# Two weighted sums of a graph network on one core: two stages with a barrier between them, against one stage with one list of tile pieces

## The reference

```python
h = (feat - mean) * rsqrt(var + EPS) * gamma + beta
feat_in, feat_out = h @ W_in + b_in, h @ W_out + b_out
a_in  = segment_sum(feat_in[src] * iw[:, None], dst, num_segments=N)
a_out = segment_sum(feat_out[dst] * ow[:, None], src, num_segments=N)
a = concatenate((a_in, a_out), axis=1)
xi, hh = a @ W_x2i + b_x2i, h @ W_h2h      # then gates: sigmoid, tanh, and the new h
```

## Time and profile before

| what | value |
|---|---|
| time, median of 3 runs | 4573.53 us (4573.35 to 4581.63) |
| the profiled execution, its own time | 4598.33 us |
| its span in the trace | 4596.4 us |
| TensorE busy | 3570.8 us, 78% of the span |
| VectorE / ScalarE / GpSimd busy | 58% / 37% / 23% |
| first sum (`gin`), matmuls | 265.3 us busy, 3674.53 us to 3939.8 us |
| second sum (`gou`), matmuls | 264.6 us busy, 3947.39 us to 4212.0 us |

### The profile page before, as it was taken

One profiled execution on the slowest core, in us unless ns is written; L12 is line 12 of the kernel. 1 busy time (PEld: TensorE's weight loads), 2 busy tenths in 40 slices (PEclk: granted clock), 3 DMA queues, 4 the chain that ended last, 5 costly groups with the idle time before them and its releaser, 6 DMA issues. The chain is left out here.

```text
span 4596.4 us, 88449 instructions
## 1 busy us (share of the span) xinstructions
PE 3570.8 (78%) x19416; PEld 2680.7 (58%) x19417; DVE 2671.9 (58%) x9145; ACT 1684.3 (37%) x5377; POOL 1077.8 (23%) x828
## 2 busy tenths in 40 slices
PE   5555548888777776999994433688999699998978
PEld 4333337776777775888883222677887344444444
DVE  7999989999887772101227888777765300000523
ACT  1555542333334441000008886777775100000110
POOL 1888888888882000000000000000000000000000
PEclk9999999999988888999995555899999899999989
DMA  3444434566667664444437654544331153542064
GB/s 104 111 111 114 111 76 126 148 187 203 193 192 246 237 242 123 134 136 127 134 98 208 188 178 130 160 126 129 112 100 61 59 210 114 179 149 66 1 256 138
DMA packets 435572, 656.94 MB, mean 143 GB/s; under 512 B 97532, under 2 KB 291767, under 8 KB 435362
## 3 DMA queue, kind: packets, MB, share of 16 engines
q1 hardware_dynamic: 354306, 526.63, 37.0%
q10 hardware_dynamic: 53040, 121.95, 7.3%
q0 software_dynamic: 28144, 7.36, 2.5%
HBM read 438.84 MB, written 216.02 MB: 142 GB/s over the span
## 5 line engine op out<-in xcount | busy, mean ns | idle before, releaser
L989 POOL DMA_INDIRECT slots<-all_B,put_index x800 | 1054.4, 1318 | 342.8 <-issue 240.4
L1724 POOL DMA_DIRECT2D out_dram<-all_B x7 | 8.6, 1224 | 2170.4 <-DVE all_B L1708 2170.4
L965 PE MATMUL put_ps<-put_right_in,put_left_in 128*128 128x125 f32 x2380 | 359.3, 303 | 144.0 <-ACT put_left_in L835 132.3
L765 DVE TENSOR_SCALAR put_hot<-all_iota_bf,put_words_in 128x125 bf16<-128x125 bf16 x2400 | 441.2, 307 | 3.3 <-DMA put_words_in<-slots 3.3
L965 PEld LDWEIGHTS put_ps<-put_right_in,put_left_in 128*128 128x128 f32 x2380 | 314.2, 208 | 171.9 <-ACT put_left_in L835 149.3
L835 ACT CAST put_left_in<-put_hot 128x640 f32 (+1 forms) x238 | 172.6, 725 | 647.3 <-issue 412.1
L1184 ACT ACTIVATE lm_raised<-lm_hot,srt_words 128x125 f32<-128x125 bf16 x1200 | 356.2, 385 | 79.7 <-DVE lm_top L1099 64.1
L2261 DVE TENSOR_TENSOR upd_pre<-upd_po,upd_bias 125x512 f32<-125x512 f32 x25 | 17.3, 692 | 629.8 <-PE upd_po L2192 629.8
L1219 PE MATMUL lm_ps<-lm_v,lm_node 125*128 x1220 | 170.0, 184 | 263.5 <-DVEq L1086 94.1
L1834 PE MATMUL att_ps<-att_right,att_left 128*125 128x125 f32 x2380 | 312.1, 285 | 68.3 <-ACT att_right L1855 64.4
L969 PE MATMUL put_ps<-put_right_out,put_left_out 128*128 128x125 f32 x2380 | 351.8, 301 | 4.0 <-DVE put_right_out L773 3.4
(11 more groups left out here) (346 smaller groups left out, 5971.1 us busy)
## 6 DMA issues: line engine op xcount, KB each, us to landing
c_T<-counts SPq DMA_DIRECT2D x255, 312.5 KB, 2.9
pair<-put_T ACTq DMA_DIRECT2D x125, 625.0 KB
hot<-put_hot SPq DMA_DIRECT2D x480, 160.0 KB
att_ring<-hot SPq DMA_DIRECT2D x240, 320.0 KB, 3.2
all_A<-in_edge_attr_dram SPq DMA_DIRECT2D x100, 448.0 KB
lm_planes<-src_rows SPq DMA_DIRECT2D x123, 320.0 KB, 3.8
counts<-put_T ACTq DMA_DIRECT2D x125, 312.5 KB
lm_hot<-hot SPq DMA_DIRECT2D x120, 320.0 KB, 3.3
```

The costliest lines, as they stand in the source:

```text
L765: ins = v.tensor_scalar(hot[:, h, t, c * S:c * S + P], k["iota_bf"][:, :], words_in[:, j, c, t:t + 1], None, ALU.is_equal)
L965: ins = t_.matmul(tile(1, c), left_in[:, c, :], right_in[:, c, :], start=False, stop=False, skip_group_check=True)
L989: nc.gpsimd.indirect_dma_start(slots, bass.IndirectOffsetOnAxis(index[:, C * g + j:C * g + j + 1], 0), stage[:, C * g + j, :], None).then_ ...
```

## The change

`phase_stream`, called twice, becomes `phase_streams`, called once with a list of the two sums. The sets of both stand in one list `jobs` of 14 entries, each with its own `H`, direction, output and group of blocks, and the loops of SP, TensorE and ScalarE run over that list. Pieces are numbered 0 to 69 through both sums, there is one ring `T` of 8 slots and one `po` (tag `gio`), and one set of semaphores. The block's barrier, the semaphore clearing and the next block's entry between the sums are gone. An unused option `load_more` and its semaphore `more` go as well. Sizes, matmuls, copies and transfers are the same ones in the same order on each engine.

```diff
-def phase_stream(nc, k, tag, H, by_dst, out, load_more=None):
+def phase_streams(nc, k, tag, sums):
...
-        sets = [range(d, min(d + SET, NB)) for d in range(0, NB, SET)]
+        jobs = [(H, by_dst, out, range(d, min(d + SET, NB))) for H, by_dst, out in sums for d in range(0, NB, SET)]
...
-        more = s.sem("more")
-
-        def piece(n, group):
+
+        def piece(n, group, by_dst):
...
             def _(sp):
-                for i, group in enumerate(sets):
+                for i, (H, by_dst, out, group) in enumerate(jobs):
                     for q in range(PIECES):
                         n = PIECES * i + q
                         if n >= HELD:
...
             def _(pe):
-                for i, group in enumerate(sets):
+                for i, (H, by_dst, out, group) in enumerate(jobs):
                     w = len(group) * P
                     if i >= 2:
                         pe.wait_ge(moved, 2 * (i - 1))
...
             def _(act):
-                for i, group in enumerate(sets):
+                for i, (H, by_dst, out, group) in enumerate(jobs):
                     act.wait_ge(used, PIECES * (i + 1))
...
-            phase_stream(nc, k, "gin", B, True, a_in)
-            phase_stream(nc, k, "gou", A, False, a_out)
+            phase_streams(nc, k, "gio", [(B, True, a_in), (A, False, a_out)])
```

More of the change, by code:

```diff
@@ L2031, in _ @@
                             tiles = k["pair"][PB * q:PB * q + PB, 1, :, group[0] * P:(group[-1] + 1) * P]
-                        sp.dma_start(piece(n, group), tiles.rearrange("d p n -> p d n")).then_inc(landed[n % HELD], 16)
-                    if i == 1 and load_more:
-                        sp.wait_ge(more, load_more(sp, more))
+                        sp.dma_start(piece(n, group, by_dst), tiles.rearrange("d p n -> p d n")).then_inc(landed[n % HELD], 16)
             @block.tensor
             def _(pe):
-                for i, group in enumerate(sets):
+                for i, (H, by_dst, out, group) in enumerate(jobs):
                     w = len(group) * P
@@ L2046, in _ @@
                             b = PB * q + t
-                            tiles = piece(n, group)[0:P, :, t * P:t * P + P] if by_dst else piece(n, group)[0:P, t, :]
+                            tiles = (piece(n, group, by_dst)[0:P, :, t * P:t * P + P] if by_dst else
+                                     piece(n, group, by_dst)[0:P, t, :])
                             for h in range(2):
```

## The result

| | before | changed |
|---|---|---|
| median, 22 runs each, us | 4574.73 (4567.66 to 4585.18) | 4567.66 (4558.29 to 4577.95) |
| ratio to before | | 0.9981, 95% interval 0.9974 to 0.9988 |
| the same again on another occasion, 15 and 11 runs | 4575.78 | 4565.40; 0.9977, interval 0.9966 to 0.9987 |

The ratio stands for 8.7 us less (0.0019 x 4574.73), with 5.5 to 11.9 as the interval; the second comparison gives 10.5. The two medians of the first comparison are only 7.1 us apart (4574.73 - 4567.66), the two means 8.7. A ratio in this document is the one on record with its interval, and it can differ from the quotient of the medians beside it, by up to 0.0006 in what follows. The forecast was 9.2 us less. So it was right in sign and size, and lay, as it said, on the line of 0.2%.

A forecast was written before the change was run, and what follows sets the result against it. It took TensorE to bound both sums, with only the hand-over to gain: 7.8 us idle + 1.4 us slow matmuls = 9.2 us off the 4573.53 us median, giving 4564.3 us; 8-in-10 range 4558 to 4572 us.

The forecast's parts named there:

- What bounds: Inside both sums TensorE is the bound; only the hand-over between the sums is at stake.
- The idle stretch: TensorE's wait between the sums goes wholly if pieces arrive in time: 7.8 us by weight loads, 7.61 idle.
- The slow matmuls: Half-clock records at the second sum's head, after the idle stretch, go: 1.4 us, 2.0 as upper end.
- The rule on the number of slow matmuls: Count after a pause varies (6, 11 or 14 in one kernel); by it the slow-matmul term is 2.5 to 5.9 us.
- The ring: Pieces 35 to 42, the second sum's first eight, land in time; cover on every piece over 20 us.
- The waits that are new: SP's waits for `used` and TensorE's for `moved` at jobs 7 and 8 cost nothing; 0.5 us by mistake.
- The clock over one long stretch: Rival: without the break the second sum's clock falls; gain gone at 0.966, 4593.6 us at 0.9; chance 0.04.
- The forecast's place: Whole-kernel gain lies on the 0.2% line: chance 0.44 faster by over 0.2%, 0.51 within, 0.05 slower.

The follow-up runs named there:

- the run with held transfers: Changed kernel, but SP issues the second sum's first piece only after all 14 copies of the first sum; 4575.28 us, ratio to before 1.0002.
- the filled pause: Kernel before, with 22 matmuls of zeros on TensorE ahead of the second sum; 4574.73 us, ratio to before 0.9996.
- the ring of 2: Changed kernel with a ring of 2 slots instead of 8; one profile, both sums 540.0 us, 12.2 more than with 8 slots.

## Why the prediction was right

*What bounds.* Right. TensorE sets the pace inside both sums, and the hand-over was the only place where time came from.

*The idle stretch, 7.8 us.* Right: 7.6 us idle are 0.0. Its parts as read from the earlier trace rows were also right by the run with held transfers: 1.2 of the 1.28 us of barrier go with the merge, the 5.9 us of transfer only with the early issue.

*The slow matmuls, 1.4 us with 2.0 as the upper end.* The mechanism is shown by the filled pause. The size was a little low: the large records' busy time fell by 253.5 - 251.7 = 1.8 us, and the starts of the 700 records say the same, 264.37 us (3947.39 to 4211.76) against 262.56 (3911.79 to 4174.35). The prediction counted by weight loads; a load runs ahead of its matmul in the flow but not at the head, so this count came out 0.4 us short. Its own count by the granted clock, 1.7 us, was nearer. With that the hand-over, from the start of the first sum's last record to that of the second's, took 272.25 us before and 262.67 after: 9.6 us less, not 9.2.

*The rule on the number of slow matmuls.* The Trainium skill (TensorE: Matmul & The Clock Gate, Part 1) has the number of slow matmuls at a kernel's start vary from run to run. The traces agree in kind: behind the pauses between the sums the 700 records took 264.4 us (twice), 264.9, 265.6 and 265.8, so 1.8 to 3.2 us more than without a pause (262.6), and at the head of the first sum 264.8 to 266.4. The larger counts that the prediction quotes, 11 and 14, did not occur: 3.2 us are at most 8 records at 0.42 us lost each. Both profiles of the kernel before have 1.8 us. That the forecast met this term within 0.4 us is in part luck: it was read from one execution, and other pauses of 3.7 to 6.5 us here cost up to 3.2.

*The ring.* Right: no piece was late. Two of its readings are wrong, and change nothing. It calls piece 42 the tightest, but that one has 3998.6 - 3939.8 = 58.8 us of cover; by its own times 35 to 37 are the tightest, with 28. And six large pieces are 7.7 MB, not 7.9. Where the cover was taken away, in the ring of 2, the wait was the one that the arithmetic gives, 3.66 for 3.6 us.

*The waits that are new.* Right: none costs anything, and the one on `moved` would cost 0.5 us if it bit.

*The clock over one long stretch.* The rival on the other side did not come: 1.00 through 484.6 us (221.8 + 262.8) without a pause.

*The forecast's place.* The measured 0.19% and 0.23% lie on either side of 0.2%, as it said. What it could not read from one profile is why its own execution was 25 us above the median; that is below.

## What to carry to other kernels

Between two stages that are bound by one engine, price the hand-over as copies + barrier + first transfer + slow matmuls; here 0.5 + 1.3 + 5.9 + 1.8 us. The barrier was the small part of it: what pays is that the next stage's first transfers are issued while the last one computes, and a common ring does that without further code. Then look for the same gap at the neighbouring hand-overs: here two were left, larger together (22 us in the medians) than the one taken.

## What the runs showed of the hardware that was not expected

- A pause of 0.52 or 2.2 to 2.3 us on TensorE (the latter behind the fillings of zeros) brought no slow records; pauses of 3.66, 4.71, 5.91, 6.50 and 7.6 us did, 1.8 to 3.2 us each. A longer pause did not cost more: 7.6 us went with 1.8 us twice, 4.71 us with 3.1.
- 22 matmuls of zeros issued beside the first transfers of a stage went with a first landing of 7.29 and 7.11 us instead of 5.86 and 5.80; 8 wide ones or 22 narrow ones with 6.64 and 6.65. In these four a load of the instruction queue lay beside the landing, in the others it did not; whether it is the cause is open.
- Executions of one kernel differ by more than the change is worth, and not in the changed stages. In the two profiles of the kernel before, TensorE's records at L965, in the stage that builds the tiles, begin alike (685.7 and 685.4 us) and end at 1724.4 and 1697.3. These 27 us are the 26.5 between the two spans (4596.4 and 4569.9). The row of the first and that of the second, in the view of one tile:

```profile
L965 PE MATMUL put_ps<-put_right_in,put_left_in x2380: 274/275/577, 685.7 to 1724.4; 128*128 128x125 f32 x199
```

```profile
L965 PE MATMUL put_ps<-put_right_in,put_left_in x2380: 274/275/577, 685.4 to 1697.3; 128*128 128x125 f32 x199
```
